# The token shift of a feed-forward layer: two matmuls and an ACT copy, or three transfers from SBUF to SBUF

## The chip, the cores and the metric

The kernel runs on one core of a Trainium2 chip. The metric is the device time of one execution in microseconds. A core has TensorE (PE, with its weight loads PEld), VectorE (DVE), ScalarE (ACT), GpSimd (POOL) and SyncE (SP); SP issues the transfers that 16 DMA engines carry out. Each engine runs its own instruction stream in order, and waits on semaphores for the others.

## The reference, cut to what matters

The program is a chain of four blocks on an input of 4 sequences x 512 tokens x 128 channels: a linear recurrence, a two-layer transformer with local attention, a second attention, and a mixture of experts. The change is in the transformer, whose layer is:

```python
def shift_token(t):
    t1, t2 = jnp.split(t, 2, axis=-1)
    t2 = jnp.pad(t2, ((0, 0), (1, 0), (0, 0)))[:, :-1]
    return jnp.concatenate([t1, t2], axis=-1)

def _layer(x, wqkv, qs, ksc, wo, lg, lb, w1, b1, w2, b2):
    ...
    x = x + o @ wo
    h = shift_token(x)
    mu = h.mean(-1, keepdims=True)
    var = h.var(-1, keepdims=True)
    h = (h - mu) / jnp.sqrt(var + 1e-05) * lg + lb
    h = h @ w1 + b1
    a, g = jnp.split(h, 2, axis=-1)
    h = a * jax.nn.gelu(g, approximate=False)
    x = x + h @ w2 + b2
    return x
```

So channels 0 to 63 of `h` are those of the token itself, and channels 64 to 127 are those of the token before it in the same sequence (zero for the first token). `shift_token` stands twice in a layer; only the second one, ahead of the layer norm of the feed-forward, is changed.

## The kernel before

Tokens lie on the 128 partitions: a sequence is `NT` = 4 tiles of 128 tokens, and `y[s]` holds [128 partitions, 4 tiles, 128 channels] of sequence s. The two layers times four sequences give 8 blocks, k = 0 to 7, and 32 tiles, i = 0 to 31. `y[0]` and `y[1]` are tensors of their own, `y[2]` and `y[3]` lie in `region_r`; the trace names them accordingly. `hs`, the shifted copy on which the layer norm works, lies in `region_b`.

**The order.** A generator, `layer_steps()`, writes out one software pipeline by hand, and each engine walks through it and emits its own part of every step. One round is one tile of attention, with the steps of neighbouring tiles interleaved; the feed-forward of block k = i // 4 - 1 is spread over the rounds after its last attention tile. Of a round i with t = i % 4 these steps matter here, in this order:

- `probs` (PE transposes, L1337; ACT exponentials, L723), `wo` (PE, L1370), `ssq` (DVE L932 and L935, POOL L567);
- t = 0: `y_att` (DVE adds the attention's output, L982, and copies channels 0 to 63 into `hs`, L986). t = 1: `ff_stats` (DVE L874 and L878: the statistics of all of `hs`);
- `vals` (PE L1351; DVE `o_out`, L972 and L975);
- t = 0: **`shift`**: PE L1381 and L1382 write channels 64 to 127, moved by one token, to PSUM bank 2, and ACT L733 copies them into `hs`;
- `heads` (PE L1308, ACT L716 and L717), `v` (PE L1300; SP moves values from SBUF to SBUF, L426 and L427), `rotsum` (DVE L957), t = 1: `ff_rstd` (POOL L545 and L547), `norm` (DVE L940);
- at most t: `up` (PE L1397; ACT gelu, L747; DVE L992), t = 1: `down` of the block before (PE L1405; DVE `y_out`, L1001);
- `scores` (PE L1320 and L1328; DVE L962 and L965), `oT` (PE L1359), `qk` (PE L1294 and L1295), t = 1: `ff_apply` (DVE L885 on `hs`), `rot`.

In the round with t = 2 the step `hnT` transposes `hs` on PE (L1389). The DVE waits for `hs_hi`, the semaphore of the upper channels, at `ff_stats`, one round after the shift was made.

**The shift.** PE multiplies by `down_one`, a 128 x 128 matrix that moves each token down one partition, and adds with `carry` the last token of a tile to the first of the next. Both matrices are made by POOL in `constants()` at the start (L551 to L556). The matmuls read `y` and wait for `y_att`.

**SP's queue.** In these layers SP issues for each tile one or two transfers of 64 rows x 2,080 bytes (L426, L427). They are needed by `vals` three rounds later. In other parts of the program it issues, among others, three transfers from `hT` with 3 rows (`ones_under`, L444: each row is 32 pieces of 256 bytes), twelve transfers of 32 pieces of 256 bytes (L493), and three transfers with `HW` = 114 rows (`w2` twice, and `b1` once, 48 bytes a row).

Of the kernel before, what the change touches and what calls it, by code (L numbers as in the profile page):

```python
# [14 lines left out]
P = 128  # L15
# [52 lines left out]
def build(nc, A, out):  # L68
    with ExitStack() as ctx:
        def sb(name, shape, dt=FP):  # L70
            return ctx.enter_context(nc.sbuf_tensor(name, shape, dt))
# [60 lines left out]
        down_one = sb("down_one", [P, P])  # L132
        carry = sb("carry", [P, P])
# [99 lines left out]
        def bank(n, width=BANK, of=1):  # L233
# [8 lines left out]
            "o_rec", "o_norm", "oT_mm", "oT_sb", "wo_mm", "y_att", "hs_lo", "hs_mm", "hs_hi", "based_y", "based",  # L242
# [146 lines left out]
        def _(sp):  # L389
# [38 lines left out]

            for what, n in layer_steps():
                if what == "v":  # L430
                    shift_values(n)
                if (what, n) == ("v", 3):
                    sp.wait_ge(M["zeros"], 1)
                    n_z = SLOT_ROWS // P * ROW // ZEROS
                    sp.dma_start(xs_dram.rearrange("(p r) c -> p (r c)", p=P).rearrange("p (n z) -> p n z", z=ZEROS),
                                 zeros.unsqueeze(1).to_broadcast([P, n_z, ZEROS])).then_inc(M["zeroed"], 16)
# [95 lines left out]
        def _(pool):  # L532
# [17 lines left out]
            def constants():  # L550
                g.memset(down_one[:, :], 0.0).then_inc(S["idn"], 1)  # L551
                g.memset(carry[:, :], 0.0).then_inc(S["idn"], 1)
                pool.wait_ge(S["idn"], 6)
                g.affine_select(out=down_one[:, :], in_=down_one[:, :], compare_op=ALU.not_equal, fill=1.0,
                                base=1, pattern=[[-1, P]], channel_multiplier=1).then_inc(S["idn"], 1)
                g.affine_select(out=carry[:, :], in_=carry[:, :], compare_op=ALU.not_equal, fill=1.0,  # L556
                                base=1 - P, pattern=[[-1, P]], channel_multiplier=1).then_inc(S["idn"], 1)
                for p in range(2):
                    g.memset(kT[p][:, :, 0:WIN], 0.0).then_inc(S["zero_p"], 1)
                    g.memset(v_off[p][0:WIN, 0, :, :], 0.0).then_inc(S["zero_p"], 1)  # L560
                    g.memset(v_al[p][:, :, :, DH:VW], 1.0).then_inc(S["zero_p"], 1)
                g.memset(zeros, 0.0).then_inc(M["zeros"], 1)
# [115 lines left out]
        def _(a):  # L678
# [51 lines left out]
            def shifted_sb(k):  # L730
                a.wait_ge(S["hs_mm"], k + 1)
                need(a, S["hnT_mm"], k)
                act_(hs[:, :, 64:P], bank(2)[:, 0:SEQ // 2].rearrange("p (t c) -> p t c", t=NT), ACT.Copy)\  # L733
                    .then_inc(S["hs_hi"], 1)

# [13 lines left out]
            for what, n in layer_steps():  # L749
# [12 lines left out]
                if what == "shift":  # L762
                    shifted_sb(n)
# [103 lines left out]
        def _(v):  # L867
# [136 lines left out]
            for what, n in layer_steps():  # L1004
# [33 lines left out]
                if what == "ff_stats":  # L1038
                    v.wait_ge(S["hs_lo"], n + 1)
                    v.wait_ge(S["hs_hi"], n + 1)  # L1040
# [203 lines left out]
        def _(pe):  # L1244
# [129 lines left out]
            def shifted(k):  # L1374
                ys = y[k % BATCH]
                if k == 0:
                    pe.wait_ge(S["idn"], 8)
                pe.wait_ge(S["y_att"], k + 1)
                claim((2,), (S["hs_hi"], k + 1))
                dst = bank(2)[:, 0:SEQ // 2].rearrange("p (t c) -> p t c", t=NT)  # L1380
                mm(dst, down_one[:, :], ys[:, :, 64:P], start=True, stop=False, skip_group_check=True)  # L1381
                mm(dst[:, 1:NT, :], carry[:, :], ys[:, 0:NT - 1, 64:P], start=False, stop=True,  # L1382
                   skip_group_check=True).then_inc(S["hs_mm"], 1)

# [24 lines left out]
            for what, n in layer_steps():  # L1409
# [22 lines left out]
                if what == "shift":  # L1432
                    shifted(n)
# [319 lines left out]
```

## Time and profile before

| | |
|---|---|
| median of 3 runs | 841.93 us (841.46 to 844.74) |
| profiled execution, its own time | 842.27 us |
| its span in the trace | 840.5 us |
| PE / PEld busy | 664.2 / 396.8 us (79% / 47% of the span) |
| DVE / ACT / POOL busy | 518.7 / 374.4 / 323.9 us |
| chain that ended last, shares of the span | PE 48%, DVE 19%, issue 14%, DMA 7%, ACT 7%, POOL 3% |
| the 8 blocks of the two layers | from about 20 to 480 us |

Busy time says how long an engine worked, the chain says which work the end waited for. The chain is followed back from the last instruction: at each step to what released it, or to the instruction before it on the same engine. Of the program's 840 us the change touches the stretch of the 8 blocks, in which the rounds repeat: blocks 1 to 6 look alike, block 0 has no feed-forward beside it, and block 7 has no attention beside it.

### The profile page before, as it was taken

To read this page: it belongs to the slowest core of one execution; us is meant where nothing else is said; L and a number is where in the kernel's file an instruction comes from. 1 tells how busy PE (TensorE), PEld (TensorE's weight loads), DVE (VectorE), ACT (ScalarE), POOL (GpSimd) and SP (SyncE) were. 2 spreads that over 40 slices of the span, in tenths; PEclk is the share of its full clock that TensorE was granted. 3 is DMA by queue.
4 is the path that set the end of the run, shared out by engine and by line. 5 is a ranking of instruction groups with operands and counts; after the bars stand their busy time and mean duration, and the time that the engine had idled before them with its cause. 6 is when DMAs were issued, how large, how long until landed. Compare 5 with 4: busy or idle time off the path is not lost.

```text
span 840.5 us, 14653 instructions
## 1 busy us (share of the span) xinstructions
PE 664.2 (79%) x5076; PEld 396.8 (47%) x5078; DVE 518.7 (62%) x915; ACT 374.4 (45%) x602; POOL 323.9 (39%) x318
## 2 busy tenths in 40 slices
PE   3566899999998999999775555789888966888881
PEld 2244666566656656665553232123233544455551
DVE  7647998778778777877733256866763553222222
ACT  0113446756575564657443542254656521333330
POOL 4544556454454445546311063200001017355552
PEclk8659999999999999999998966689999988899996
DMA  8103210100010010001000137636326101122224
GB/s 253 28 13 117 81 27 21 27 21 13 21 28 18 16 27 14 20 21 27 15 1 1 45 79 154 152 100 143 109 79 229 49 4 47 49 62 60 59 60 119
DMA packets 35507, 50.57 MB, mean 60 GB/s; under 512 B 5965, under 2 KB 24697, under 8 KB 34169
## 3 DMA queue, kind: packets, MB, share of 16 engines
q1 hardware_dynamic: 33401, 45.58, 20.9%
q0 software_dynamic: 2048, 4.21, 1.5%
q8 instruction: 38, 0.62, 0.3%
q14 instruction: 20, 0.16, 0.1%
HBM read 30.31 MB, written 11.83 MB: 50 GB/s over the span
## 4 chain that ended last, share of the span: by engine, by line
PE 48%; DVE 19%; issue 14%; DMA 7%; ACT 7%; POOL 3%; SPq 1%; POOLq 0%; DVEq 0%; ACTq 0%
PE ps L1603 5%; PE ps L1397 5%; DVE region_b L965 5%; DVE smx L962 5%; PE ps L1351 4%; PE ps L1337 4%; PE ps L1308 4%; PE ps L1328 3%; DVE mneg L1139 3%; PE ps L1405 3%; PE ps L1461 3%; DMA region_b<-parts_dram 2%; PE ps L1616 2%; ACT pts L723 2%; PE ps L1545 2%
## 5 line engine op out<-in xcount | busy, mean ns | idle before, releaser
L567 POOL TENSOR_TENSOR rnorm<-ssum_c,neg_half 128x16 f32<-128x16 f32 x32 | 93.8, 2932 | 157.0 <-DVE ssum_c L935 157.0
L1139 DVE TENSOR_REDUCE mneg<-ps 128x2 f32<-128x1024 f32 x64 | 75.3, 1217 | 33.1 <-PE ps L1532 33.1
L579 POOL TENSOR_TENSOR region_r<-region_b,region_d 128x512 f32<-128x512 f32 x64 | 80.8, 1283 | 30.3 <-DVE region_b L940 29.5
L813 ACT ACTIVATE region_r<-ps 128x1024 f32<-128x1024 f32 x64 | 64.4, 1024 | 54.2 <-PE ps L1545 54.1
L545 POOL TENSOR_TENSOR var_eps<-mv,eps 128x4 f32<-128x4 f32 x20 | 5.0, 250 | 184.4 <-DVE mv L878 184.4
L1222 DVE TENSOR_TENSOR region_r<-region_r,ps 128x256 f32<-128x256 f32 x48 | 20.2, 422 | 77.0 <-ACT region_r L845 45.5
L670 POOL DMA_INDIRECT y_dram<-region_r x48 | 50.0, 1043 | 44.3 <-DVE region_r L1231 25.9
L1603 PE MATMUL ps<-region_a,region_r 128*128 x96 | 55.4, 660 | 13.2 <-issue 12.5
L684 ACT ACT_TABLE_LOAD x49 | 62.9, 1283 | 1.6 <-PEq L1745 0.7
L699 ACT ACTIVATE region_a<-ps 128x1024 f32<-128x1024 f32 x32 | 33.0, 1032 | 63.0 <-PE ps L1295 63.0
L1397 PE MATMUL ps<-region_a,region_d 128*114 128x512 f32 x96 | 49.4, 640 | 12.8 <-ACT region_a L717 8.6
L992 DVE SCALAR_TENSOR_TENSOR region_b<-ps,b,region_a 114x512 f32<-114x512 f32 x24 | 18.0, 751 | 53.5 <-ACT region_a L747 53.5
L962 DVE TENSOR_REDUCE smx<-ps 128x8 f32<-128x1024 f32 x32 | 39.2, 1224 | 15.7 <-PE ps L1328 15.3
L1337 PE MATMUL ps<-ident,region_b 128*128 128x128 f32 x256 | 35.0, 280 | 15.3 <-DVE region_b L965 15.3
L1337 PEld LDWEIGHTS ps<-ident,region_b 128*128 128x128 f32 x256 | 27.4, 141 | 40.0 <-DVE region_b L965 40.0
L1294 PE MATMUL ps<-region_d,hT 128*128 128x512 f32 x64 | 36.1, 648 | 11.0 <-DVE region_b L940 7.8
L716 ACT ACTIVATE region_a<-ps 128x512 f32<-128x512 f32 x32 | 19.1, 597 | 57.3 <-PE ps L1308 57.3
L839 ACT ACTIVATE region_r<-ps 128x128 f32<-128x128 f32 x48 | 13.3, 278 | 70.0 <-PE ps L1596 70.0
L932 DVE TENSOR_REDUCE ssum<-region_a 128x16 f32<-128x1024 f32 x32 | 38.8, 1213 | 9.2 <-ACT region_a L699 9.2
L1351 PE MATMUL ps<-region_b,pts 128*64 128x65 f32 x512 | 36.6, 226 | 8.6 <-ACT pts L723 8.5
L940 DVE TENSOR_TENSOR region_b<-ps,rnorm 128x1024 f32<-128x1024 f32 x32 | 39.0, 1218 | 6.0 <-POOL rnorm L567 6.0
L1532 PE MATMUL ps<-region_b 96*128 96x512 bf16 x96 | 34.0, 451 | 9.4 <-DMA region_b<-parts_dram 4.4
(214 smaller groups left out, 1549.9 us busy)
## 6 DMA issues: line engine op xcount, KB each, us to landing
region_a<-in_wgu SPq DMA_DIRECT2D x16, 512.0 KB, 3.7
region_b<-region_a SPq DMA_DIRECT2D x56, 130.0 KB, 2.3
region_d<-in_wd SPq DMA_DIRECT2D x4, 1024.0 KB, 5.8
xs_dram<-region_a SPq DMA_DIRECT2D x1, 3354.0 KB, 12.9
pts<-xs_dram SPq DMA_DIRECT2D x50, 64.5 KB
parts_dram<-region_b SPq DMA_DIRECT2D x8, 384.0 KB, 2.6
region_b<-parts_dram SPq DMA_DIRECT2D x6, 384.0 KB, 6.9
region_d<-in_wqkv SPq DMA_DIRECT2D x2, 768.0 KB, 8.6
```

The lines of the kernel that those rows point to most:

```text
L567: g.tensor_tensor(rnorm[:, :], ssum_c[n % 2][:, :], neg_half[:, :], ALU.pow).then_inc(S["rnormed"], 1)
L579: g.tensor_tensor(dst, src, tab, ALU.mult).then_inc(S["rot_bb"], 1)
L670: g.indirect_dma_start(out=y_dram[:, :], out_offset=bass.IndirectOffsetOnAxis(ap=slot_id[:, r:r + 1], axis=0), in_=ys[r], in_offset=None). ...
L684: act_(warm[:, :], ones_f[:, 0:1], function).then_inc(S["warm"], 1)
L813: act_(dst, bank(l1_bank[what, b, i], of=2), ACT.Exp).then_inc(T["ex"], 1)
L962: d.tensor_reduce(smx[n % 2][:, :], sc, AX.X, ALU.max).then_inc(S["smax"], 1)
L965: d.tensor_tensor(sdiff[n % 2], sc, smx[n % 2][:, :].unsqueeze(2).to_broadcast([P, HEADS, P]), ALU.subtract).then_inc(S["diffed"], 1)
L1139: d.tensor_reduce(mneg[b % 2][:, 2 * i:2 * i + 2], bank(l1_bank[what, b, i], of=2) .rearrange("p (q t) -> p q t", q=2), AX.X, ALU.max, neg ...
L1337: last = tr(bank(6 + h // 4)[:, (h % 4) * P:(h % 4 + 1) * P], sdiff[n % 2][:, h, :], ident[:, :])
L1351: last = mm(ps[w * WIN:(w + 1) * WIN, c0:c0 + VW], pts[n % 2][:, j, w * WIN:(w + 1) * WIN], vals[:, t, h, :], start=True, stop=True)
L1397: last = mm(ps[0:HW, (6 + g) * BANK:(7 + g) * BANK], w1[k // BATCH][:, g, c, :], hnT, start=True, stop=True)
L1603: mm(bank(2 + t % 2), xsT[t % 2], wgu[:, bass.ds(e, 1), :].rearrange("p a n -> p (a n)"), start=True, stop=True).then_inc(M["gu_mm"], 1)
```

## The change

The two constant matrices, the two matmuls and the ACT copy go. In their place SP issues three transfers at the step `shift`, which write channels 64 to 127 of `hs` directly: one of 127 partitions x 4 tiles x 64 channels, from each partition to the next; one of the three rows that cross from the last partition of a tile to the first of the next tile; and one row of zeros for the first token. `hs_hi` then counts 48 a block. SP waits for `y_att` and, because `hs` is overwritten, for the transposes of the block before (`hnT_mm`), which PE waited for through ACT's copy before.

```diff
-            "o_rec", "o_norm", "oT_mm", "oT_sb", "wo_mm", "y_att", "hs_lo", "hs_mm", "hs_hi", "based_y", "based",
+            "o_rec", "o_norm", "oT_mm", "oT_sb", "wo_mm", "y_att", "hs_lo", "hs_hi", "based_y", "based",
...
+            def shift_tokens(k):
+
+                ys = y[k % BATCH]
+                sp.wait_ge(S["y_att"], k + 1)
+                need(sp, S["hnT_mm"], k)
+                if k == 0:
+                    sp.wait_ge(M["zeros"], 1)
+                sp.dma_start(hs[1:P, :, 64:P], ys[0:P - 1, :, 64:P]).then_inc(S["hs_hi"], 16)
+                sp.dma_start(hs[0:1, 1:NT, 64:P], ys[P - 1:P, 0:NT - 1, 64:P]).then_inc(S["hs_hi"], 16)
+                sp.dma_start(hs[0:1, 0, 64:P], zeros[0:1, 0:64]).then_inc(S["hs_hi"], 16)
+
             for what, n in layer_steps():
+                if what == "shift":
+                    shift_tokens(n)
                 if what == "v":
                     shift_values(n)
...
             def constants():
-                g.memset(down_one[:, :], 0.0).then_inc(S["idn"], 1)
-                g.memset(carry[:, :], 0.0).then_inc(S["idn"], 1)
-                pool.wait_ge(S["idn"], 6)
-                g.affine_select(out=down_one[:, :], in_=down_one[:, :], compare_op=ALU.not_equal, fill=1.0,
-                                base=1, pattern=[[-1, P]], channel_multiplier=1).then_inc(S["idn"], 1)
-                g.affine_select(out=carry[:, :], in_=carry[:, :], compare_op=ALU.not_equal, fill=1.0,
-                                base=1 - P, pattern=[[-1, P]], channel_multiplier=1).then_inc(S["idn"], 1)
...
-            def shifted_sb(k):
-                a.wait_ge(S["hs_mm"], k + 1)
-                need(a, S["hnT_mm"], k)
-                act_(hs[:, :, 64:P], bank(2)[:, 0:SEQ // 2].rearrange("p (t c) -> p t c", t=NT), ACT.Copy)\
-                    .then_inc(S["hs_hi"], 1)
...
                 if what == "ff_stats":
                     v.wait_ge(S["hs_lo"], n + 1)
-                    v.wait_ge(S["hs_hi"], n + 1)
+                    v.wait_ge(S["hs_hi"], 16 * 3 * (n + 1))
                     norm_stats(ln_no[what, n], hs)
...
-            def shifted(k):
-                ys = y[k % BATCH]
-                if k == 0:
-                    pe.wait_ge(S["idn"], 8)
-                pe.wait_ge(S["y_att"], k + 1)
-                claim((2,), (S["hs_hi"], k + 1))
-                dst = bank(2)[:, 0:SEQ // 2].rearrange("p (t c) -> p t c", t=NT)
-                mm(dst, down_one[:, :], ys[:, :, 64:P], start=True, stop=False, skip_group_check=True)
-                mm(dst[:, 1:NT, :], carry[:, :], ys[:, 0:NT - 1, 64:P], start=False, stop=True,
-                   skip_group_check=True).then_inc(S["hs_mm"], 1)
```

On PE, before, the round that ends block 0 runs from `wo` (L1370) through `vals` (L1351, 16 rows of each of two kinds in turn) to the shift and on to `heads` (L1308), `v` (L1300) and `scores` (L1320, L1328):

```order
L1370 MATMUL ps<-region_d,oT1 128x128 x4
L1351 MATMUL ps<-region_b,pts0 64x65
L1351 MATMUL ps<-region_a,pts0 64x65
...
L1381 MATMUL ps<-y0,down_one 128x256
L1382 MATMUL ps<-y0,carry 128x192
L1308 MATMUL ps<-ident,region_r 128x128 x8
L1300 MATMUL ps<-region_d,hT1 128x512
L1320 MATMUL ps<-mask_b,ident_b 128x512 x2
```

In the changed kernel (its lines stand 4 lower here) the same place reads:

```order
L1366 MATMUL ps<-region_d,oT1 128x128 x4
L1347 MATMUL ps<-region_b,pts0 64x65
L1347 MATMUL ps<-region_a,pts0 64x65
...
L1304 MATMUL ps<-ident,region_r 128x128 x8
L1296 MATMUL ps<-region_d,hT1 128x512
L1316 MATMUL ps<-mask_b,ident_b 128x512 x2
```

`heads` follows directly on `vals`; nothing else on PE has moved.

On SP the queue around the same place, in the changed kernel, with its waits (L424 and L425 are the value transfers, L426 and L427 before):

```order
L424 DMA region_b<-region_a 64x520 [waits v_off_in2,v_sb]
L425 DMA region_b<-region_a 64x520
L434 DMA region_b<-y 127x4x64 [waits moe_zeros,y_att]
L435 DMA region_b<-y 1x3x64
L436 DMA region_b<-region_a 1x16x4
L424 DMA region_b<-region_a 64x520 [waits v_off_in3,v_sb]
```

The three new transfers stand between the value transfers of two rounds; before, these followed on each other.

## Rows read from the trace of the kernel before

**Rows 1.** Chain that ended last: start us, us, what; block 3's shift round, next round

```profile
256.31 0.63 PE ps L1381 x2
256.94 0.33 PE ps L1382 x2
257.26 0.89 PE ps L1308 x8
...
268.98 1.04 PE ps L1308 x8
```

**Rows 2.** Timeline, ACT and POOL: start us, us, engine, line, operation, [idle before <-releaser]

```profile
257.30 0.39 ACT L733 ACTIVATE region_b<-ps 128x256 f32<-128x256 f32 x1 [2.40 <-PE ps L1382]
```

```profile
28.29 2.91 POOL L567 TENSOR_TENSOR rnorm<-ssum_c,neg_half 128x16 f32<-128x16 f32 x1 [7.44 <-DVE ssum_c L935]
```

**Rows 3.** Timeline, DVE, block 3: from y_att to the scores of the next round

```profile
255.07 0.68 DVE L982 TENSOR_TENSOR region_r<-region_r,ps 128x512 f32<-128x512 f32 x1
...
267.77 0.88 DVE L874 BATCH_NORM_STATS2 stats<-region_b 128x6 f32<-128x128 f32 x4
...
271.00 1.22 DVE L940 TENSOR_TENSOR region_b<-ps,rnorm 128x1024 f32<-128x1024 f32 x1
274.22 0.69 DVE L1001 TENSOR_TENSOR region_r<-region_r,ps 128x512 f32<-128x512 f32 x1 [2.01 <-PE ps L1405]
275.72 1.23 DVE L962 TENSOR_REDUCE smx<-ps 128x8 f32<-128x1024 f32 x1 [0.81 <-PE ps L1328]
```

**Rows 4.** Timeline, DVE, block 0: the same three places

```profile
113.01 0.68 DVE L982 TENSOR_TENSOR y<-y,ps 128x512 f32<-128x512 f32 x1
```

```profile
123.36 0.87 DVE L874 BATCH_NORM_STATS2 stats<-region_b 128x6 f32<-128x128 f32 x4
...
127.99 1.22 DVE L962 TENSOR_REDUCE smx<-ps 128x8 f32<-128x1024 f32 x1 [0.18 <-PE ps L1328]
```

**Rows 5.** Timeline, all engines, block 7: the end of the layers

```profile
448.48 0.69 DVE L982 TENSOR_TENSOR region_r<-region_r,ps 128x512 f32<-128x512 f32 x1 [2.47 <-PE ps L1370]
...
450.59 3.07 PE L1397 MATMUL ps<-region_a,region_d 128*114 128x512 f32 x4
...
455.08 0.86 DVE L874 BATCH_NORM_STATS2 stats<-region_b 128x6 f32<-128x128 f32 x4
...
456.71 1.02 POOL L547 TENSOR_TENSOR rstd<-var_eps,neg_half 128x4 f32<-128x4 f32 x1
...
458.87 3.16 DVE L885 TENSOR_SCALAR region_b<-region_b,mv,rstd 128x128 f32<-128x128 f32 x4
```

**Rows 6.** DMA issues of the whole program: count, KB each, us to landing

```profile
region_b<-region_a SPq DMA_DIRECT2D x56, 130.0 KB, 2.3
...
region_d<-in_w SPq DMA_DIRECT2D x2, 171.0 KB
...
region_b<-hT SPq DMA_DIRECT2D x2, 24.0 KB
...
region_r<-hT SPq DMA_DIRECT2D x1, 24.0 KB
...
b<-in_b SPq DMA_DIRECT2D x1, 5.3 KB
```

**Rows 7.** DMA packets of the whole program, and of the stretch 259 to 263 us

```profile
DMA packets 35507, 50.57 MB, mean 60 GB/s; under 512 B 5965, under 2 KB 24697, under 8 KB 34169
```

```profile
DMA packets 160, 0.27 MB, mean 67 GB/s; under 512 B 32, under 2 KB 32, under 8 KB 160
...
q1 hardware_dynamic: 160, 0.27, 30.9%
```

**Rows 8.** DMA, 485 to 486; 40 slices of 486.6 to 488; 40 slices of 23.2 to 23.8 us

```profile
DMA packets 78, 0.02 MB, mean 20 GB/s; under 512 B 78, under 2 KB 78, under 8 KB 78
```

```profile
GB/s 15 15 15 15 15 15 15 15 15 15 15 22 15 15 15 22 15 15 15 15 15 19 26 22 0 0 0 0 0 0 0 0 0 0 0 0 0 0 0 0
```

```profile
GB/s 0 34 0 34 0 2 1 2 1 2 1 1 18 18 18 18 18 18 18 18 0 0 0 0 0 0 0 0 0 0 0 0 0 0 0 0 0 0 0 0
```

More of the change, by code:

```diff
@@ L131, in build @@
         ident_b = sb("ident_b", [P, P], BF)
-        down_one = sb("down_one", [P, P])
-        carry = sb("carry", [P, P])
         mask_b = sb("mask_b", [P, 2, P], BF)
@@ L761, in _ @@
                     outputs_sb(n)
-                if what == "shift":
-                    shifted_sb(n)
                 if what == "hnT":
@@ L1431, in _ @@
                     project_o(n)
-                if what == "shift":
-                    shifted(n)
                 if what == "hnT":
```

## The prediction, made before the changed kernel was run

> **What bounds the kernel now.** I read the chain that ended last over the blocks first, then DVE's timeline at the two ends of the shift, then the DMA views, since the change trades engine work for transfers. In a round that ends a block, the chain runs vals, both shifting matmuls, `heads` [rows 1]: the shift is on the chain by its place in PE's queue, not because anyone there needs its result. `heads` waits for nothing else, so what stands between it and `vals` delays the round. ACT's copy is not on the chain: it takes 0.39 us after 2.40 us of idling, and ends before the first copy of `heads` could start [rows 2]. The result of the shift is needed only by `ff_stats`. In block 3 `y_att` ends at 255.75 and `ff_stats` starts at 267.77 [rows 3], 12.0 us later, when DVE comes to it; it never waits for `hs_hi` before.
>
> **What the change removes.** PE: 0.63 + 0.33 us go, but `heads` takes 1.04 us where it follows directly on `vals` and 0.89 us behind the shift [rows 1], so a round gains 0.63 + 0.33 + 0.89 - 1.04 = 0.81 us. Nothing is next in line there: DVE idles 0.81 us ahead of the scores and 2.01 us ahead of `y_out` [rows 3]. Blocks 0 to 6 gain up to 0.81 us each, 5.7 us in all. Block 7 gains more. There PE waited for `y_att`, shifted, and only then began `up` at about 450.8; `up` needs neither and can start when `wo` ends, just before `y_att` starts at 448.48 [rows 5]: 2.3 us. POOL's four instructions for the matrices run in a stretch where it idles 7.44 us ahead of its next work [rows 2], so they are worth nothing. With a shift that costs nothing the kernel would gain 5.7 + 2.3 = 8.0 us.
>
> **What it adds.** Three transfers a block on SP's queue. Behind SP's new wait stand only the value transfers of the same round, which come after `y_att` anyway and are read three rounds later, so neither the wait nor the issue time costs anything. What counts is when the large transfer lands, since DVE's `ff_stats` now waits for it, and behind it in DVE's queue stand `o_out`, `rotsum`, `norm`, `y_out` and the scores, thus the whole chain. It moves 127 x 4 = 508 pieces of 256 bytes.
>
> *How many DMA engines carry it.* The value transfer has 64 rows, and two of them leave 160 packets, 128 of data and 32 small ones [rows 7]: 16 small packets each, one completion from each of 16 engines. Transfers with other row counts can be counted over the whole program. It has 280 transfers, of which three have 3 rows (24 KB) and three have 114 (171 KB twice, 5.3 KB once) [rows 6]. Of its 5,965 packets under 512 B [rows 7], 1,554 are data: five loads with 128 small rows and the gate weights with 128, 114 rows of `b1`, 288 and 384 pieces of 256 bytes from `hT`, which is 768 + 114 + 672. The 4,411 that are left are completions. The 274 other transfers make 274 x 16 = 4,384 of them, so the six make 27, which is 3 x 3 + 3 x 6. So 3 rows go to 3 engines, 114 rows to 6, 64 rows to 16: the largest number up to 16 that divides the rows. 127 is prime. The large transfer runs on **one** engine, all 508 pieces in a line.
>
> The Trainium skill speaks against this change in the same way (DMA: Bandwidth & Descriptors, "Why a DMA increments its semaphore by 16 and not by 1"): it gives this rule, and names 127 partitions as a case of one engine. The trace's count agrees; by the opposite assumption, 16 engines, the sum is that of the first rival below.
>
> *How long a piece takes.* The part that doesn't grow: the value transfer lands 2.3 us after its issue [rows 6]; its engines are busy 30.9% of 4 us x 16 for 128 packets, about 0.15 us each, and each carries 4, so 2.3 - 0.6 = 1.7 us are fixed. For a piece of 256 bytes there are these rows. The 3-row transfers move 78 pieces in 1 us on three engines [rows 8], 26 an engine: 38 ns. When the first engine is done, the other two go on at 15 GB/s [rows 8], 17 ns a piece together, 34 ns an engine. And at 23.5 us one engine alone works off the last load from HBM, packets of 272 bytes at 18 GB/s [rows 8]: 15 ns. The first is the nearest in kind (256 bytes, SBUF to SBUF, long lines) but shared by three; the last is one engine alone, but with eight pieces that had been queued for long. Ends of the range: 15 and 38 ns. From three engines to two the time of a piece fell by 4 ns; for one alone I take 28 ns, a value between 34 and 15, nearer to the rows of the same kind. The landing is then 1.7 + 508 x 0.028 = 15.9 us after `y_att`.
>
> **The sum.** *Blocks 1 to 6*, by block 3: landing at 255.75 + 15.9 = 271.7. From the start of `ff_stats` to the end of `norm` DVE needs 272.22 - 267.77 = 4.45 us, `y_out` 0.7 more, since PE is done by then [rows 3]. The scores start at 271.7 + 5.2 = 276.9 instead of 275.72: +1.2 us, the gain of 0.81 included; six of them, +7.1. *Block 0*: landing at 113.69 + 15.9 = 129.6; 4.5 us later, at 134.1, the scores, which started at 127.99 [rows 4]: +6.1. *Block 7*: there is no attention for cover. Landing at 449.17 + 15.9 = 465.1. Statistics and POOL's inverse root take 457.73 - 455.08 = 2.65 us [rows 5], so `ff_apply` starts at 467.8 instead of 458.87: +8.9. All that follows depends on it. Together +22 us: 841.9 + 22 = **864 us**. The profiled execution took 842.27 us, its span 840.5; the terms are differences, so I add them to the median.
>
> The landing has three limits, and they show what decides. Without loss it may come, after `y_att`, 13.9 us later in blocks 1 to 6 (24 ns a piece), 9.0 us in block 0 (14 ns), and 4.7 us in block 7 (6 ns).
>
> **Rivals.**
> (a) *The transfer spreads over 16 engines* all the same. Then 32 pieces an engine, at 38 ns 1.2 us, land after 2.9 us, within all three limits: 841.9 - 8.0 = 834 us. Against it: the count of completions. Chance 0.05.
> (b) *One engine, at its own pace.* At 15 ns the landing comes after 9.3 us. Blocks 1 to 6 keep 0.81 us each, -4.9; block 0 stands at 123.0 + 4.5, -0.5; block 7 at 458.5 + 2.7, +2.3. The sum is -3.1: 839 us, and at 20 ns 844. This is the case in which the change isn't slower, and it holds below about 18 ns. For it: the 18 GB/s of one engine, and that 78 pieces a microsecond are 13 ns each if three engines share one path, which a single one would have to itself. Against it: two engines should then share the same 13 ns, and they were slower, 17. Chance 0.3.
> The skill has a rule for it (the same page, "Why small descriptors are slow"): 256 bytes take 8 beats and 3 cycles of overhead, an estimate of 13 ns at the fabric's clock; the time by it is (b)'s, 837 to 839 us. No row here shows one engine with a long line of such pieces.
> (c) *One engine, as slow as each of the three.* 38 ns: landing after 21.0 us. Blocks 1 to 6: 276.8 + 5.2, +6.2 each, 37; block 0: +11.2; block 7: +14.0. Sum +62: 904 us. PE would then idle some 6 us before the scores of each block, and if its granted clock falls for that, the time lies above this sum; no row here prices it. For it: the nearest row in kind. Against it: those engines weren't alone. Chance 0.28.
>
> **How the numbers follow.** Forecast, 23 to 34 ns a piece, 850 to 890 us: 0.37. (a) 0.05, (b) 0.3, (c) 0.28. The range must take in most of (b) and (c): 837 to 908 us. A measurement of this kernel can tell about 0.5%, 4.2 us, from no change. Faster by more needs (a), or (b) at its lowest: 0.08. Same is most of (b), 0.26. Slower is the rest, 0.66.
>
> **What would show it.** In the profile after: 508 packets of 256 bytes in a line at a DMA share of one engine in 16; a wait of DVE at L874 for a DMA, longest in block 7, then block 0; `heads` directly behind `vals`; `ff_stats` in block 3 about 16 us behind `y_att`. If DVE's wait appears only in blocks 0 and 7, (b) is right. If the packets under 512 B show 16 completions for the large transfer, or it lands within 4 us, my count was wrong and (a) holds. If PE's clock falls after each wait, the time lies above the sum.

## The result and the profile after

The changed kernel takes 846.46 us (median of 9 runs, 843.99 to 849.27), the kernel before 842.91 us (9 runs beside it, 840.89 to 845.39). The ratio is 1.0045, 95% interval 1.0025 to 1.0065: slower by 3.6 us between the medians (3.8 by the ratio), at the edge of what can be told from no change, and far from the 864 us of the forecast. Ratios and their intervals, here and below, come from the fast runs of both kernels measured beside each other, and differ by up to 0.25% from the quotient of the two medians. The profiled execution of the changed kernel took 847.46 us, its span 845.6.

The count of engines was right. Packets of the whole program, after:

```profile
DMA packets 39883, 51.62 MB, mean 61 GB/s; under 512 B 10341, under 2 KB 29073, under 8 KB 38545
```

Against [rows 7] there are 10,341 - 5,965 = 4,376 more small packets, 547 a block: 508 pieces, 3 of the carried row and 16 of the zero row, and 20 completions, 1 + 3 + 16. The large transfer has one completion: one engine. How fast that engine goes stands in the DMA view of block 7, 445 to 453 us in 40 slices:

```profile
GB/s 0 0 0 0 15 14 17 12 15 13 15 18 15 18 18 18 18 18 18 19 18 17 17 15 15 15 17 15 15 15 15 15 17 15 15 15 15 15 15 18
DMA packets 454, 0.12 MB, mean 14 GB/s; under 512 B 454, under 2 KB 454, under 8 KB 454
```

The line flows without a break at 15 to 18 GB/s. In the records of the packets, 511 pieces (the 508 and the three of the carried row) take 8.17 us from the first start to the last end, 445.82 to 453.99, **16.0 ns** each, where the prediction took 28. (The expectations below reckon with 15.8.)

Block 7 in the timeline (start us, us, engine, line, operation, idle before and its releaser); first SP's three issues, then DVE, then PE:

```profile
444.44 0.75 SPq L434 DMA_DIRECT2D region_b<-region_r  x1
445.23 7.01 SPq L435 DMA_DIRECT2D region_b<-region_r  x1
452.28 0.54 SPq L436 DMA_DIRECT2D region_b<-region_a  x1
```

```profile
443.72 0.69 DVE L978 TENSOR_TENSOR region_r<-region_r,ps 128x512 f32<-128x512 f32 x1 [2.46 <-PE ps L1366]
...
455.04 0.87 DVE L870 BATCH_NORM_STATS2 stats<-region_b 128x6 f32<-128x128 f32 x4 [6.50 <-DMA region_b<-region_a]
...
457.81 2.55 DVE L881 TENSOR_SCALAR region_b<-region_b,mv,rstd 128x128 f32<-128x128 f32 x2 [0.91 <-POOL rstd L558]
```

```profile
460.92 1.12 PE L1374 MATMUL ps<-ident,region_b 128*128 128x128 f32 x4 [9.33 <-DVE region_b L881]
462.91 3.76 PE L1382 MATMUL ps<-region_a,region_d 128*114 128x512 f32 x4 [0.87 <-ACT region_a L739]
468.32 3.73 PE L1382 MATMUL ps<-region_a,region_d 128*114 128x512 f32 x4 [1.66 <-DVE region_b L988]
473.70 3.73 PE L1382 MATMUL ps<-region_a,region_d 128*114 128x512 f32 x4 [1.65 <-DVE region_b L988]
```

Three things are to be seen. First, the issue of the carried row (L435), which takes 0.76 us in the experiment with short lines (e1_sixteen), stands 7.01 us: SP doesn't get it off while the long line is being worked off, and the zero row (L436) is issued only 8 us after `y_att`. The last of the three transfers lands so that `ff_stats` starts 10.6 us after `y_att` ends (444.41 to 455.04); DVE has waited 6.50 us for it. The late issue is hardly what decides this. The long line itself flows until 453.95 us, when the zero row's packets are nearly all done (DMA view of 453 to 454.2 us in 40 slices):

```profile
GB/s 17 17 17 17 9 26 9 17 17 17 9 17 17 17 17 11 27 11 19 18 18 9 17 17 17 17 9 26 9 17 17 9 9 0 0 0 0 0 0 0
```

In the records of the semaphores, 15 of the zero row's 16 signals have come by 453.89 us, and the last three signals of all come at 454.60, 454.78 and 454.96, behind the end of the long line. Second, PE idles for 9.33 us. Third, the three groups of `up` behind that take 3.73 to 3.76 us each. In the kernel before the same three are:

```profile
463.60 3.45 PE L1397 MATMUL ps<-region_a,region_d 128*114 128x512 f32 x4 [0.87 <-ACT region_a L741]
468.71 1.94 PE L1397 MATMUL ps<-region_a,region_d 128*114 128x512 f32 x4 [1.66 <-DVE region_b L992]
472.32 1.94 PE L1397 MATMUL ps<-region_a,region_d 128*114 128x512 f32 x4 [1.66 <-DVE region_b L992]
```

1.94 us is a group at 2.4 GHz, 3.73 to 3.76 us one at 1.2. The granted clock of 440 to 480 us (us, PE busy, granted clock, DMA share, GB/s), before and then after:

```profile
440.00:480.00 40.00, 24.36 (x123) 0.88 0.00 0
```

```profile
440.00:480.00 40.00, 20.84 (x62) 0.66 0.02 4
```

0.88 and 0.66 are 9.5 and 27.3 us at half clock. In block 0 DVE waits for the transfer too, 1.72 us:

```profile
122.19 0.87 DVE L870 BATCH_NORM_STATS2 stats<-region_b 128x6 f32<-128x128 f32 x4 [1.72 <-DMA region_b<-region_a]
```

In block 6 it waits 0.65 us (the view names no releaser there; the last signal of the transfers comes just before, at 408.52 us):

```profile
408.60 0.87 DVE L870 BATCH_NORM_STATS2 stats<-region_b 128x6 f32<-128x128 f32 x4 [0.65 <-issue]
```

In blocks 1 to 5 it never does, but not by much: in block 3 the last signal comes at 263.17 us, 0.7 us before `ff_stats`. Block 3, the rows that answer to [rows 3], and `heads`, now directly behind `vals`:

```profile
251.97 0.68 DVE L978 TENSOR_TENSOR region_r<-region_r,ps 128x512 f32<-128x512 f32 x1
...
263.86 0.87 DVE L870 BATCH_NORM_STATS2 stats<-region_b 128x6 f32<-128x128 f32 x4
...
267.10 1.22 DVE L936 TENSOR_TENSOR region_b<-ps,rnorm 128x1024 f32<-128x1024 f32 x1
270.32 0.69 DVE L997 TENSOR_TENSOR region_r<-region_r,ps 128x512 f32<-128x512 f32 x1 [2.01 <-PE ps L1390]
271.82 1.23 DVE L958 TENSOR_REDUCE smx<-ps 128x8 f32<-128x1024 f32 x1 [0.81 <-PE ps L1324]
```

```profile
253.14 1.09 PE L1304 MATMUL ps<-ident,region_r 128*128 128x128 f32 x8
```

`y_att` to `ff_stats` is 11.9 us, before 12.7: the round is 0.8 us shorter, and the waits of 2.01 and 0.81 us ahead of `y_out` and the scores are what they were.

**A ledger.** The runs of a kernel scatter by 5 us and more, and the time at half clock behind 490 us scatters too: 75 to 100 us in the traces. The timeline of the 8 blocks is steadier: between two starts of `y_att` the two traces of a kernel agree within 0.1 us, but for the round of block 6. So I cut this stretch by the start of `y_att` of blocks 0, 1, 6 and 7 and by PE's first matmul behind it (`ps<-ident,y`), in each trace, in us. That matmul opens the program's second attention; the table, the expectations and the text call what it opens "the second layer" or "layer 2", and the 8 blocks with both transformer layers "the layer". An (m) marks kernels in which POOL still builds the two shift matrices.

| kernel | to y_att(0) | 0 to 1 | 1 to 6 | 6 to 7 | 7 to layer 2 | layer 2 begins | clock 440-480 |
|---|---|---|---|---|---|---|---|
| before (m) | 113.0 | 43.6 | 246.4 | 45.5 | 38.1 | 486.6 | 0.88 |
| before, second trace (m) | 111.8 | 43.6 | 246.4 | 46.6 | 38.1 | 486.6 | 0.88 |
| after | 110.9 | 44.2 | 242.3 | 46.4 | 46.0 | 489.7 | 0.66 |
| after, second trace | 111.2 | 44.2 | 242.3 | 46.4 | 46.0 | 490.1 | 0.66 |
| e1_sixteen | 111.4 | 42.8 | 242.3 | 47.5 | 39.7 | 483.6 | 0.77 |
| e2_last_mm (m) | 112.5 | 44.2 | 242.3 | 46.4 | 43.7 | 489.0 | 0.66 |
| e3_only_last (m) | 112.6 | 43.6 | 246.4 | 45.6 | 44.2 | 492.3 | 0.76 |
| e4_warm | 112.0 | 44.2 | 242.3 | 46.4 | 43.9 | 488.8 | 0.83 |
| e5_sixteen_busy | 111.8 | 42.9 | 242.3 | 46.5 | 35.9 | 479.4 | 0.92 |
| e6_last_mm_busy (m) | 112.5 | 44.3 | 242.2 | 47.6 | 37.8 | 484.5 | 1.00 |
| e7_before_busy (m) | 112.3 | 43.6 | 246.4 | 48.4 | 37.8 | 488.5 | 1.00 |
| e8_half_pieces | 110.8 | 46.3 | 242.2 | 45.7 | 45.1 | 490.1 | 0.74 |
| e9_after_busy | 111.7 | 44.4 | 242.3 | 46.5 | 40.2 | 485.1 | 1.00 |
| e12_zero_first | 111.5 | 42.9 | 242.3 | 47.6 | 35.9 | 480.2 | 0.94 |

After against before, first traces: -2.1, +0.6, -4.1, +0.9, +7.9, together +3.2 us; second traces +3.5. Blocks 1 to 5 give 0.82 us each, as forecast (1 to 6 in the table); block 0 and above all block 7 take it back. The spans of the same two pairs differ by 5.1 and 5.0 us: the other 1.5 to 1.9 us arise behind the start of the second layer, where nothing was changed, and no run here explains them. The rounds of block 6 (6 to 7) scatter with the clock: 45.5 us in the first trace of the kernel before, and 46.6 us in the second, which has one more stretch of 3.4 us at half clock, at 412.1 us.

### The profile page after: what moved, and what is told of

It reads as the page before. It is cut to its first block, busy times and chain, and to the rows that moved or that the text cites. A ratio compares the mean times of both kernels' runs of the same rounds, so it can differ in the third digit from the quotient of the medians.

```text
span 845.6 us, 14593 instructions
## 1 busy us (share of the span) xinstructions
PE 660.5 (78%) x5045; PEld 390.3 (46%) x5046; DVE 515.5 (61%) x915; ACT 370.8 (44%) x594; POOL 322.9 (38%) x314
## 2 busy tenths in 40 slices
DMA packets 39883, 51.62 MB, mean 61 GB/s; under 512 B 10341, under 2 KB 29073, under 8 KB 38545
## 4 chain that ended last, share of the span: by engine, by line
PE 49%; DVE 18%; issue 13%; DMA 8%; ACT 6%; SPq 3%; POOL 3%; POOLq 0%; DVEq 0%; ACTq 0%
PE ps L1382 6%; PE ps L1586 5%; DVE smx L958 5%; DVE region_b L961 4%; PE ps L1333 4%; PE ps L1347 4%; PE ps L1304 4%; PE ps L1324 3%; PE ps L1444 3%; DVE mneg L1135 3%; PE ps L1390 2%; PE ps L1528 2%; DMA region_b<-parts_dram 2%; PE ps L1599 2%; ACT pts L727 2%
## 5 line engine op out<-in xcount | busy, mean ns | idle before, releaser
L1382 PE MATMUL ps<-region_a,region_d 128*114 128x512 f32 x96 | 53.6, 686 | 12.8 <-ACT region_a L721 8.6
L1290 PE MATMUL ps<-region_d,hT 128*128 128x512 f32 x64 | 36.2, 649 | 10.6 <-DVE region_b L936 8.2
L928 DVE TENSOR_REDUCE ssum<-region_a 128x16 f32<-128x1024 f32 x32 | 38.7, 1211 | 8.6 <-ACT region_a L703 8.6
L1347 PE MATMUL ps<-region_b,pts 128*64 128x65 f32 x512 | 35.9, 223 | 8.6 <-ACT pts L727 8.5
```

The lines of the kernel that those rows point to most:

```text
L1347: last = mm(ps[w * WIN:(w + 1) * WIN, c0:c0 + VW], pts[n % 2][:, j, w * WIN:(w + 1) * WIN], vals[:, t, h, :], start=True, stop=True)
L1382: last = mm(ps[0:HW, (6 + g) * BANK:(7 + g) * BANK], w1[k // BATCH][:, g, c, :], hnT, start=True, stop=True)
```

## The experiments

**One engine or sixteen.** The large transfer split so that 112 rows go to 16 engines and 15 rows to 15; nothing else changes.

```
-sp.dma_start(hs[1:P, :, 64:P], ys[0:P - 1, :, 64:P]).then_inc(S["hs_hi"], 16)
+sp.dma_start(hs[1:113, :, 64:P], ys[0:112, :, 64:P]).then_inc(S["hs_hi"], 16)
+sp.dma_start(hs[113:P, :, 64:P], ys[112:P - 1, :, 64:P]).then_inc(S["hs_hi"], 16)
...
-v.wait_ge(S["hs_hi"], 16 * 3 * (n + 1))
+v.wait_ge(S["hs_hi"], 16 * 4 * (n + 1))
```

> The 127-row transfer of every block is split into one of 112 rows and one of 15, which divide over 16 and 15 engines; all else as in the changed kernel (846.5 us, before 842.9). Theory 1: the loss is the long line of 508 pieces on one DMA engine, which makes ff_stats wait in blocks 0 and 7 and leaves PE idle in block 7. Then the shift lands 3 to 4 us after y_att, DVE never waits at ff_stats in blocks 0 to 6, all seven keep 0.81 us, block 7 keeps its 2.3 us: 8 us faster than before, 835 us. Theory 2: the loss has nothing to do with the landing (it is the traffic, or the later stages): no faster than before, 843 to 847 us.

Measured: 841.03 us against 844.96, ratio 0.993 (0.9907 to 0.9953). The expectation (8 us faster than before, 835 us) had the sign right and not the size: 3.9 us were measured between the medians, 5.9 by the ratio. Block 0 to 1 is 1.4 us shorter than with one engine, block 7 6.3 us, so the single engine costs both. But block 7 still took 39.7 us, with all three `up` groups at 3.73 to 3.76 us, although PE idled only 4.62 us ahead of them: something was missing.

**Which block gives and which takes.** Two hybrids: transfers in blocks 0 to 6 and the matmuls with ACT's copy in block 7, and the other way round. Core of the edit, for the first:

```
 if what == "shift" and n < 7: shift_tokens(n)        # SP
 if what == "shift" and not (n < 7): shifted(n)       # PE, and shifted_sb(n) on ACT
```

> Blocks 0 to 6 by the changed kernel's transfers, block 7 by the two matmuls and the ACT copy of the kernel before. Theory 1: in the profiled runs blocks 0 to 6 gained 4.3 us between the first and the last y_att (from -2.14 to -6.4 against before), and all the loss came behind y_att of block 7. So this kernel keeps the 4 to 5 us and loses nothing behind: 838 us. Theory 2 (the loss arises in the later stages whatever block 7 does): 846 us.

Measured: 845.7 us, ratio 1.0004 (0.9983 to 1.0024). A miss. The ledger shows why: 1 to 6 has its 4.1 us, but 7 to the second layer takes 43.7 us instead of 38.1, though it runs the very same instructions as before, because the clock there is 0.66 and not 0.88. No transfer is waited for in this block, and PE idles exactly as long ahead of the transposes as in the kernel before, 3.85 us:

```profile
462.32 1.11 PE L1404 MATMUL ps<-ident,region_b 128*128 128x128 f32 x4 [3.85 <-DVE region_b L898]
```

So the clock of block 7 can fall without the wait for the transfer.

> The reverse: blocks 0 to 6 by matmuls, block 7 alone by the changed kernel's transfers. Theory 1: only the loss of block 7, without the gains: 846.5 + 4.5 = 851 us. Theory 2: near before, 843 us.

Measured: 850.0 us, ratio 1.0062 (1.0039 to 1.0086), as expected. Block 7 alone costs 44.2 - 38.1 = 6.1 us. `ff_apply` starts 3.7 us later, as in the changed kernel, which leaves 2.4 us for the clock; the `up` groups take 3.76, 3.65 and 1.94 us behind an idle time of 10.95 us, the longest of all.

**Is it the clock?** The first look puts eight matmuls that nobody reads behind `down(6)`, where PE idles 9.33 us.

```
+def warm_up(k):
+    for _ in range(8):
+        mm(bank(0), ident[:, :], hT[1][:, :], start=True, stop=True)
...
+if (what, n) == ("down", BLOCKS - 2):
+    warm_up(n)
```

> The changed kernel, with 8 matmuls of 512 columns on PE behind the down projection of block 6, whose result nobody reads; they fill the 9.3 us in which PE idles while the transfer of block 7 is under way (0.86 us each at full clock, 6.9 us). The landing and the wait of DVE stay. Theory 1a: of the loss in block 7 the part behind ff_apply, 4.2 us in the profiled runs (L1382 3.7 us a group in place of 1.94), is PE's granted clock, which fell in that idle time. Then the groups take 1.94 us, and the kernel 842 us or less. Theory 1b: the clock has nothing to do with it: 846.5 us, with the groups still at 3.7 us.

Measured: 845.32 us against 844.96, ratio 1.0003 (0.9973 to 1.0034), where 842 us or less was expected: by the ledger the direction (block 7 takes 43.9 us instead of 46.0), not the size, and the ratio's interval overlaps that of the changed kernel. They stopped 2.7 us short of the wait's end, and two of three `up` groups still ran slow (3.76, 3.40, 1.94 us). The next four kernels (and e12 below) put 29 such matmuls (34 in e9, with 13 behind `down(6)`) in the waits of the last rounds.

```
+def keep_busy(count):
+    pe.wait_ge(S["normed"], NTILES)
+    for _ in range(count):
+        mm(bank(0), ident[:, :], hT[1][:, :], start=True, stop=True)
...
+idle = {("heads", NTILES - 2): 2, ("heads", NTILES - 1): 2, ("oT", NTILES - 3): 3,
+        ("oT", NTILES - 2): 3, ("oT", NTILES - 1): 3, ("up", HC * BLOCKS - 5): 2,
+        ("down", BLOCKS - 2): 8, ("up", HC * BLOCKS - 4): 2, ("up", HC * BLOCKS - 3): 2,
+        ("up", HC * BLOCKS - 2): 2}
+if (what, n) in idle:
+    keep_busy(idle[what, n])
```

> The 127 rows go as 112 and 15 (16 and 15 engines), and PE gets 29 matmuls more whose result nobody reads, all placed where PE waits: 2 or 3 behind heads, the transposes of the outputs and up in the last rounds, 8 behind down(6), 2 behind each of the first three up of block 7. Without them the split alone took 841.0 us, 0.993 of the kernel before, with PE at half clock from 454.5 to 471.6 us and three up groups of block 7 at 3.7 instead of 1.9 us. Theory A, the clock gave back what the transfers gained: the half-clock windows between 400 and 472 us go, three up groups gain 1.8 us each, the time falls by 4 to 6 us against the split alone: ratio 0.986 to 0.988, 832 to 834 us. Theory B, the clock is not what limits there and the gain was lost elsewhere: ratio 0.993 or, since the matmuls cost issue time, above.

> Transfers in blocks 0 to 6, the two matmuls and ACT's copy in block 7, with the same 29 idle matmuls. Without them it took as long as the kernel before (ratio 1.0004), though 0.81 us in each of blocks 1 to 6 should be won. Theory A (given back by the clock): the windows of half clock at 421 and 435 us and in the tail go, 27.3 us of half clock between 440 and 480 us become 7 or less, ratio 0.992 to 0.995, 837 to 840 us. Theory B (the gain isn't there at all): ratio stays at 1.000.

> The kernel before with the same 29 idle matmuls. Theory A: its clock hardly fell in these rounds (0.7 us at half clock from 110 to 440 us, 9.5 us from 440 to 480), so there is little to win: ratio 0.997 to 1.000. If the traced execution of before was an untypical one and its clock falls in the tail as often as that of the other kernels, the ratio is 0.993 to 0.996, and then the clock doesn't tell the kernel with transfers from the one with matmuls. Theory B: ratio 1.000 or above.

> The changed kernel (one engine for 127 rows) with the idle matmuls, 13 instead of 8 behind down(6) so that they cover the longer wait. Clock theory: PE stays at full clock to the end of block 7, y_att(7) starts near 443.5 us, from there 35.9 us as in the split kernel with idle matmuls plus the 6.3 us that ff_stats starts later (455.04 - 443.72 against 448.91 - 443.93): the first matmul of the second layer at about 485.8 us, 2.7 us before that of the kernel before with idle matmuls (488.50) and 3.9 us before that of the changed kernel (489.74); ratio to before 0.996 to 0.999. This is the sum of the prediction with 15.8 ns a piece and a full clock. If the transfer costs something that neither the landing nor the clock shows: first matmul of the second layer at 488 us or later, ratio 1.003 or above.

| kernel with idle matmuls | us | ratio to before | without them |
|---|---|---|---|
| e5, sixteen engines | 836.79 | 0.9898 (0.9862 to 0.9933) | 0.9930 |
| e6, matmuls in block 7 | 841.96 | 0.9973 (0.9945 to 1.0002) | 1.0004 |
| e7, kernel before | 846.65 | 1.0017 (0.9985 to 1.0049) | 1 |
| e9, changed kernel | 840.99 | 0.9966 (0.9945 to 0.9987) | 1.0045 |

The idle matmuls bring nothing to the kernel before, and 0.3 to 0.8% to the three with transfers. Only for e9 do the intervals with and without them stand apart; for e5 and e6 the ledger carries the reading. e5 came short of its own expectation, 832 to 834 us, and e6's half clock from 440 to 480 us is gone, as expected, but its ratio is above the 0.992 to 0.995 expected. e9 is the sharpest case: its wait for the transfer is as long as ever, and only the clock differs. Its block 7, DVE, then PE, then the windows:

```profile
456.16 0.87 DVE L870 BATCH_NORM_STATS2 stats<-region_b 128x6 f32<-128x128 f32 x4 [8.16 <-DMA region_b<-region_a]
```

```profile
450.90 11.32 PE L1388 MATMUL ps<-hT,ident 128*128 128x512 f32 x26
462.06 0.65 PE L1374 MATMUL ps<-ident,region_b 128*128 128x128 f32 x4
463.58 1.97 PE L1382 MATMUL ps<-region_a,region_d 128*114 128x512 f32 x4 [0.87 <-ACT region_a L739]
...
467.21 1.94 PE L1382 MATMUL ps<-region_a,region_d 128*114 128x512 f32 x4
...
470.81 1.94 PE L1382 MATMUL ps<-region_a,region_d 128*114 128x512 f32 x4
```

```profile
440.00:480.00 40.00, 34.81 (x127) 1.00 0.04 9
```

From `ff_stats` to the second layer it needs 485.06 - 456.16 = 28.9 us, the changed kernel 489.74 - 455.04 = 34.7: 5.8 us in which, apart from the idle matmuls in PE's gaps, nothing but the clock is different. The expectation gave the sum 485.8 us and 0.996 to 0.999; it came as 485.06 and 0.9966. e7's 0.997 to 1.000 came as 1.0017: the three idle matmuls ahead of the last `wo` make `y_att(7)` wait for it 4.15 us instead of 2.47, as in all five kernels with idle matmuls, and its round of block 6 has a stretch at half clock at 412.6 us besides (6 to 7: 48.4 us instead of 45.5). Against e7 the layer of e6 is 4.0 us shorter, about the 4.1 of 1 to 6.

The Trainium skill (TensorE: Matmul & The Clock Gate, "HAM oscillation — how this bites in real kernels") says that a wait for a DMA between groups of matmuls lets the clock fall, so that the next group starts at the low one. e3 agrees: with the transfer in block 7 alone, 2.4 us are lost behind the wait. But the wait is not needed for it: e2 has no such wait and loses 5.6 us in the same place, and e1, with a PE idle time half as long as the changed kernel's, has all three groups at half clock. e2 differs from the kernel before only in the rounds ahead of block 7, so the clock of block 7 depends on something in those rounds; on what, no run here settles.

**By piece or by byte?** The large transfer as two with half the columns each, 1,016 pieces of 128 bytes.

```
-sp.dma_start(hs[1:P, :, 64:P], ys[0:P - 1, :, 64:P]).then_inc(S["hs_hi"], 16)
+sp.dma_start(hs[1:P, :, 64:96], ys[0:P - 1, :, 64:96]).then_inc(S["hs_hi"], 16)
+sp.dma_start(hs[1:P, :, 96:P], ys[0:P - 1, :, 96:P]).then_inc(S["hs_hi"], 16)
```

> The large transfer as two of 127 rows with half the columns each: 1,016 pieces of 128 bytes in place of 508 of 256, the bytes the same. If both run on the same engine and a piece has its time whatever its size (15.8 ns): 16 us for the line, landing about 18.7 us after y_att, over all three landing limits of the prediction (13.9, 9.0 and 4.7 us): blocks 1 to 6 lose 4.8 us each, block 0 9.7, block 7 14.0, together +52 us, 895 us. If time goes by bytes: 8 us for the line, 10.6 us, 846 us as with whole pieces. Between (by the Trainium skill, DMA: Bandwidth and Descriptors, Why small descriptors are slow, 4 beats and 3 cycles, an estimate of 7/11 of the time of 256 bytes): 10.2 us for the line, landing 12.9 us after y_att, blocks 1 to 6 still unharmed, blocks 0 and 7 about 2.2 us later each, 851 us. If the two transfers run on two engines: as with whole pieces or earlier.

Measured: 848.21 us against 844.35, ratio 1.006 (1.0031 to 1.0089). SP, the DMA view of 447 to 456 us, and DVE in block 7:

```profile
446.50 4.39 SPq L435 DMA_DIRECT2D region_b<-region_r  x1
450.94 4.75 SPq L436 DMA_DIRECT2D region_b<-region_r  x1
```

```profile
DMA packets 947, 0.12 MB, mean 13 GB/s; under 512 B 947, under 2 KB 947, under 8 KB 947
```

```profile
457.45 0.87 DVE L871 BATCH_NORM_STATS2 stats<-region_b 128x6 f32<-128x128 f32 x4 [8.46 <-DMA region_b<-region_a]
```

947 packets in 9 us are 9.5 ns each. It is neither one time a piece (16.0) nor one a byte (8.0), but between, and both transfers run on the same engine, else the line would be half as long. Landing: 457.45 - 445.67 = 11.8 us after `y_att`. DVE now waits about 0.5 us at `ff_stats` of blocks 1 to 5 too, but the rounds get no longer for it (1 to 6: 242.2 us); block 0 to 1 grows by 2.1 us. The expectation's middle case was the right one (12.9 us and 851 us expected).

**Does the issue order matter?** e5 with the zero row issued before the wait for `y_att`, so that three issues stand behind `y_att` instead of four.

```
 need(sp, S["hnT_mm"], k)
+sp.dma_start(hs[0:1, 0, 64:P], zeros[0:1, 0:64]).then_inc(S["hs_hi"], 16)
 sp.wait_ge(S["y_att"], k + 1)
```

> The split kernel with idle matmuls, where the transfer of the zero row is issued before the wait for y_att, so three issues stand behind y_att instead of four. If issuing is what the landing waits for in the split kernel (ff_stats of block 7 started 4.98 us behind y_att, though an engine has 32 pieces or about 0.5 us of work): it starts 4.2 to 4.5 us behind y_att, the second layer at 478.8 instead of 479.4 us, time 0.6 us below the split kernel with idle matmuls, ratio 0.989. If the transfer time is what it waits for: 4.98 us as before, ratio 0.990.

Measured: 837.52 us against 843.66, ratio 0.9911 (0.9879 to 0.9943), no difference to e5 that can be told; the second layer begins at 480.2 us, not at 478.8 as expected. `ff_stats` of e12 and of e5:

```profile
448.55 0.87 DVE L871 BATCH_NORM_STATS2 stats<-region_b 128x6 f32<-128x128 f32 x4 [1.08 <-DMA region_b<-region_r]
```

```profile
449.96 0.87 DVE L871 BATCH_NORM_STATS2 stats<-region_b 128x6 f32<-128x128 f32 x4 [3.28 <-DMA region_b<-region_a]
```

It starts 4.26 us behind the start of `y_att`, in e5 6.47, in e1 4.98. So the issues do limit the landing of the split kernel: one issue less brings 0.7 us against e1. The 6.47 us of e5 are another matter: 15 of the zero row's 16 signals have come by 448.39 us and the last comes at 449.88, while one packet of 16 KB on the queue of instruction loads (q8) takes from 447.88 to 448.83. That the two share an engine is likely, not shown. The layer ends no earlier in e12 (35.9 us in both): the eight idle matmuls behind `down(6)` occupy PE until about 456.5 us in e5 and 457.2 in e12, the transposes follow directly on them, and so they now hide the gain. That a smaller number would give it back wasn't tried.

**Were the two traces typical?** One more trace of each kernel.

> The kernel before, for a second trace. If its clock in the last rounds is typical of the kernel, the second layer begins at 486 to 488 us, with 10 us or less at half clock from 440 to 480 us. If the first trace was a lucky one, it begins at 490 us or later with up groups of block 7 at 3.7 us, and then the kernel with transfers is the faster one in this layer.

> The changed kernel, for a second trace. If its long wait in block 7 is what lets the clock fall: PE idles about 9.3 us ahead of the transposes of block 7 and three up groups take 3.7 us again, second layer from 489 to 490 us. If it was chance: the up groups take 1.9 us and the second layer begins at about 485 us.

Measured: the second layer begins at 486.60 us (842.8 us in all) and at 490.12 us (847.7 us); `up` groups of 3.49, 1.94 and 1.94 us, and of 3.76, 3.73 and 3.73 us behind an idle time of 9.36 us. The clock's fall in block 7 came in both traces of the changed kernel, and in neither of the kernel before.

## Why the prediction was wrong, step by step

**The step that failed** is "How long a piece takes": "for one alone I take 28 ns, a value between 34 and 15, nearer to the rows of the same kind". It measured 16.0 ns. The row of one engine alone (18 GB/s, [rows 8]) was nearest, though its packets came from HBM; the rows of two and three engines were slower for each of them, and likeness of kind misled me. Why an engine is slower beside others, no run here shows. With the landing at the 10.6 us measured and not at 15.9, the prediction's own sum falls from +22 to -4.9 + 0.8 + 3.6 = -0.5 us. The time of a piece is the term of the sum that was mis-sized; the fixed part of the landing was 0.8 us too small besides (below). Rival (b), at 0.3, had the pace right, but not the outcome: it gave 839 to 844 us and called this "the case in which the change isn't slower". The change is slower, and what the sum lacks for that is above all the clock. The range held the time, which is partly luck: between 837 and 908 us there was room for one term too large and another left out.

Step by step:

- *Count of engines*: one, exactly.
- *Gain of 0.81 us a block*: 0.82 in blocks 1 to 5, not to be told in block 6. The landing limit of 13.9 us wasn't reached; DVE waits in blocks 0 and 7, and 0.65 us in block 6.
- *Block 0*: with 15.9 us the sum was +6.1; with the landing of 10.6 us it is +0.8. Measured +0.6.
- *Block 7*: +8.9 becomes +3.6. Measured from `y_att` to `ff_apply`: 14.09 us against 10.39, +3.7.
- *"1.7 us are fixed"*: too small by 0.8 us, for 10.6 us is not 1.7 + 508 x 0.016 = 9.8. From the end of `y_att` to the first piece 1.4 us pass, from the last piece to the line's signal 0.65, and 0.36 more until the two signals behind it and 0.1 to `ff_stats` are through, 2.5 us together.
- *"neither the wait nor the issue time costs anything"*: nearly so here. The issue of the carried row is held for 7 us, which the prediction did not see, but the last signals come behind the end of the long line, which an earlier issue of the short ones would hardly have moved; no run tests it with the long line. In the split kernel the issues do count (e12).
- *POOL's four instructions "are worth nothing"*: wrong, they are worth 0.8 to 1.0 us. I looked at POOL's idle time, and the loss was on DVE (last section).
- *The clock*: named only beside rival (c) and at the end, and priced nowhere. It is the second half of the loss in block 7: after `ff_apply` the changed kernel takes 31.9 us to the second layer and the kernel before 27.7, +4.2 us, of which the three `up` groups are 11.2 - 7.3 = 3.9.

Together: -1.0 (POOL, mean of the traces), +0.6, -4.1, +3.7, +4.2 are +3.4 us up to the second layer, where the two pairs of traces show +3.2 and +3.5; the measured difference of the times is +3.6 to 3.8. Block 6 is left out of it, at 0 between its +0.9 (first traces) and -0.3 (second traces). That the sum comes near the whole time is in part chance, since the traces lose another 1.5 to 1.9 us behind it.

The arithmetic of rival (a) can be tested by e5 and e7, the split kernel and the kernel before with the same idle matmuls: 488.5 - 479.4 = 9.1 us, where the prediction said 8.0. But of the 9.1, 0.5 fall before `y_att(0)`, and about 1.1 are the stretch of e7 at half clock at 412.6 us, by the price of such a stretch in the two traces of the kernel before. The other 7.5 are 0.7 (block 0), 4.1, 0.8 and 1.9 (block 7, where the prediction said 2.3).

What stays open: why the clock falls in block 7 where no transfer is waited for (e2); what the stretches at half clock cost that the changed kernel has in the rounds of block 6 (3.4 us each, at 419.7 and 433.4 us; the kernel before has one at 439.3), by an estimate 1.7 us, from the 45.5 us before less the gain of 0.8 against the 46.4 measured; and the scatter of 2 us up to `y_att(0)`, of which POOL explains half.

## What to carry to other kernels

The transfer of 127 rows, a prime number, was a line on one engine: split as 112 + 15, the kernel goes from 1.0045 to 0.993. Price PE's clock as well as the wait when work moves off PE: the matmuls behind the change can run at half clock, with a wait ahead of them (e3) or without one (e2). In e9 idle matmuls in PE's gaps gave 5.8 us back, and e5 (836.79 us, 0.990) beats both kernels, but the same matmuls are worth nothing where the clock hardly fell (e7). A block's cover decides, not the average: eleven microseconds of other work hide the transfer in blocks 1 to 5, and blocks 0 and 7, with less, give the gain back.

## What the runs showed of the hardware

- One DMA engine alone moved 256-byte pieces from SBUF to SBUF in 16.0 ns each and 128-byte pieces in 9.5 ns (e8). The Trainium skill (DMA: Bandwidth & Descriptors, "Why small descriptors are slow (HBM only)") gives 8 beats and 3 cycles for 256 bytes, an estimate of 13 ns; by the same rule half the bytes would be 7 cycles, an estimate. The ratio 7/11 = 0.64 is near the measured 0.59, the level is a quarter higher. The same section says that transfers from SBUF to SBUF don't suffer from small pieces, which the prediction left out; here, on one engine, they did: 16 GB/s with 256 bytes and 13.5 with 128.
- While a line of 508 pieces is worked off on one engine, SP's next issue of a small transfer stands 6.6 to 7.0 us; with lines of 28 pieces an engine an issue takes 0.6 to 1.1 us.
- POOL's memsets can hold DVE's instructions up. At the start DVE applies the norm to `y` in eight equal pieces. The first four take 1.08 us together, the last four 3.04 before and 2.19 after:

```profile
17.95 3.04 DVE L885 TENSOR_SCALAR y<-xr,mv,rstd 128x128 f32<-128x128 f32 x4 [0.51 <-POOL rstd L547]
```

```profile
17.58 2.19 DVE L881 TENSOR_SCALAR y<-xr,mv,rstd 128x128 f32<-128x128 f32 x4 [0.51 <-POOL rstd L558]
```

The longest single piece is 2.37 us before and 1.46 after, where the median of the eight is 0.34 and 0.42 (line, count, ns min/median/max):

```profile
L885 DVE TENSOR_SCALAR y<-xr,mv,rstd x8: 314/344/2370, 16.4 to 18.8; 128x128 f32<-128x128 f32 x8
```

```profile
L881 DVE TENSOR_SCALAR y<-xr,mv,rstd x8: 314/417/1455, 16.0 to 19.3; 128x128 f32<-128x128 f32 x8
```

The four end just behind POOL's row of work, at 20.99 and at 19.77 us. That row lasts from 17.77 to 20.84 us with the two shift matrices, and from 17.39 to 19.62 without. First and last of it, before, then after:

```profile
17.77 0.20 POOL L551 MEMSET down_one<- 128x128 f32 x1
...
20.32 0.52 POOL L562 MEMSET region_a<- 128x516 f32 x1
```

```profile
17.39 0.31 POOL L563 MEMSET region_a<- 128x256 f32 x1
...
18.96 0.66 POOL L566 MEMSET region_a<- 128x516 f32 x1
```

Behind the four pieces in DVE's queue stands a copy to `hT` (L928, L924 after), which starts at 21.02 and at 19.80 us, and PE's next matmuls wait for it. In the six traces with the matrices `y_att(0)` starts at 111.8 to 113.0 us, mean 112.5, in the eight without at 110.8 to 112.0, mean 111.4; the six include three with transfers (e2, e3, e6), so it is not the transfers. The Trainium skill (SBUF — State Buffer, "SBUF: two separate sides") says that the port pair that DVE and GpSimd share is an exclusive lock: a GpSimd instruction and a DVE instruction in a mode with two ports block each other for a whole instruction. The trace agrees in the long pieces beside POOL's memsets; in which mode these DVE instructions run, and so whether this is the cause, no run here shows.
